# Far key products of a delta-rule scan moved from VectorE to GpSimd, in a one-core transformer block

## What is computed

```python
q, k, v, beta = split(layernorm(x) @ w_qkvb + b_qkvb)      # 16 heads of 16
k = k / max(norm(k), 1e-6)
def step(S, inp):                                          # S: 16x16 per batch and head
    retrieval = einsum("bhij,bhj->bhi", S, k_t)
    S = S + einsum("bhi,bhj->bhij", beta_t * (v_t - retrieval), k_t)
    return S, einsum("bhij,bhj->bhi", S, q_t)
x = x + (x + scan_out @ w_out + b_out)
```

## Time and profile before

| | before |
|---|---|
| time of 3 runs: median (lowest to highest) | 1209.48 us (1209.47 to 1211.79) |
| the profiled execution, its time | 1210.13 us |
| its span, first to last instruction | 1208.4 us |
| DVE busy | 999.9 us (83%) |
| PE busy | 947.1 us (78%) |
| ACT busy | 632.2 us (52%) |
| POOL busy | 438.6 us (36%) |

### The profile page before, as it was taken

The page is one execution under the profiler, slowest core; times in us unless marked ns, Lnnn a source line. Parts: engine busy times, 40 slices in busy tenths (PEclk is TensorE's granted clock), DMA queues, the critical chain, the costliest instruction groups (busy, mean ns, idle before and its releaser), DMA issues.

```text
span 1208.4 us, 19595 instructions
## 1 busy us (share of the span) xinstructions
PE 947.1 (78%) x6080; PEld 707.4 (59%) x6087; DVE 999.9 (83%) x3021; ACT 632.2 (52%) x1476; POOL 438.6 (36%) x647
## 2 busy tenths in 40 slices
PE   1468999999999999999999998899887601794156
PEld 1357777777777777777777776666655400341034
DVE  3578999999999999999999998855666788798877
ACT  1244555555555655655556553446476440684097
POOL 2413543535435445354353441314467640000000
PEclk9688999999999999999999998899998955797579
DMA  9430000000000000000000000133300000000012
GB/s 198 59 105 1 9 7 6 10 6 7 9 5 10 6 6 10 6 9 7 6 10 5 8 8 5 27 110 105 93 13 1 1 0 0 1 1 1 1 49 92
DMA packets 30263, 30.51 MB, mean 25 GB/s; under 512 B 7248, under 2 KB 25552, under 8 KB 30160
## 3 DMA queue, kind: packets, MB, share of 16 engines
q1 hardware_dynamic: 30160, 29.26, 9.5%
HBM read 20.85 MB, written 4.19 MB: 21 GB/s over the span
## 4 chain that ended last, share of the span: by engine, by line
DVE 61%; PE 24%; issue 9%; ACT 4%; POOL 1%; DMA 1%; DVEq 0%; SPq 0%; ACTq 0%; POOLq 0%
PE ps L1543 6%; DVE arena L993 6%; DVE arena L996 6%; DVE work L1477 4%; DVE arena L975 4%; DVE arena L974 4%; PE ps L1705 3%; DVE arena L984 3%; DVE arena L987 3%; DVE arena L1039 3%; PE psY L1726 3%; DVE work L901 2%; DVE arena L1046 2%; PE psX L1726 2%; DVE arena L997 2%
## 5 line engine op out<-in xcount | busy, mean ns | idle before, releaser
L482 POOL TENSOR_TENSOR arena<-arena 128x256 f32<-128x256 f32 x32 | 23.3, 728 | 367.2 <-DVE arena L975 367.2
L572 ACT ACTIVATE arena<-ps 128x512 f32<-128x512 f32 x128 | 72.9, 596 | 49.2 <-PE ps L1601 48.7
L537 ACT ACTIVATE arena<-ps,nparity 32x256 f32<-32x256 f32 x124 | 51.1, 457 | 81.8 <-PE ps L1543 81.4
L457 POOL TENSOR_SCALAR_AFFINE_SELECT arena<-arena 128x2048 f32<-128x2048 f32 x32 | 92.1, 2877 | 2.2
L1601 PE MATMUL ps<-work 32*128 32x256 f32 x512 | 91.8, 400 | 0.8 <-ACT w2t L642 0.7
L1543 PE MATMUL ps<-work,arena 128*128 128x64 f32 x496 | 68.1, 295 | 30.6 <-DVE work L1008 30.0
L1543 PEld LDWEIGHTS ps<-work,arena 128*128 128x128 f32 x496 | 63.4, 207 | 37.7 <-DVE work L1008 37.7
L1566 PE MATMUL psG<-arena 128*128 128x512 f32 x128 | 73.8, 659 | 1.9 <-DVE arena L1039 1.9
L468 POOL TENSOR_TENSOR work<-work 128x16 f32<-128x16 f32 x96 | 51.2, 533 | 58.1 <-DVEq L1068 53.1
L1601 PEld LDWEIGHTS ps<-work 32*128 32x128 f32 x512 | 61.1, 184 | 17.5 <-issue 10.1
L993 DVE TENSOR_TENSOR arena<-arena 128x256 f32<-128x256 f32 (+1 forms) x96 | 66.4, 692 | 3.3
(11 more groups left out here) (294 smaller groups left out, 2640.2 us busy)
## 6 DMA issues: line engine op xcount, KB each, us to landing
arena<-in_mask_BxSxS_ik SPq DMA_DIRECT2D x8, 1024.0 KB, 6.7
arena<-in_x SPq DMA_DIRECT2D x32, 128.0 KB, 11.9
arena<-in_ctx SPq DMA_DIRECT2D x8, 512.0 KB, 4.2
xs<-arena SPq DMA_DIRECT2D x256, 16.0 KB, 1.8
out<-xs SPq DMA_DIRECT2D x32, 128.0 KB, 1.7
arena<-in_L_ffn_w SPq DMA_DIRECT2D x2, 1024.0 KB, 8.8
arena<-in_L_attn_w_qkvb SPq DMA_DIRECT2D x1, 1024.0 KB, 8.8
work<-in_L_attn_w_out SPq DMA_DIRECT2D x1, 256.0 KB, 4.7
```

What stands on the lines that cost most here:

```text
L457: G.affine_select(out=pairs, in_=pairs, compare_op=ALU.is_ge, fill=0.0, base=0, pattern=[[0, NH], [-CT, B], [0, CT]], channel_multiplier=1 ...
L572: A.activation(attn[j % 2][:, r * 512:(r + 1) * 512], ps[(2, 0)[r % 2]][:, :], ACT.Copy).then_inc(att_out, 1)
```

## The change

`far_products` is taken out of DVE's program and written into POOL's. On POOL it is called at the end of each iteration j, for chunk j + 2, behind `key_norms(j + 3)`. It waits for the same two semaphores (`k_ready`, `g1_mm`), does the same multiplication from the same keys into the same columns of `PR`, and increments the same `prod1`. The helpers `over_s` and `over_t` are written out. Nothing else is changed; the orders of PE, ACT and SP stay.

```diff
@@ GpSimd @@
+            def far_products(m):
+                pool.wait_ge(k_ready, m + 1)
+                pool.wait_ge(g1_mm, 2 * m)
+                key = kq[m % 4][:, 0:CW].rearrange("p (q t) -> p q t", t=16)
+                late = key[:, :, 8:16].rearrange("p q (t a) -> p q t a", a=1).broadcast_to([P, NH, 8, 8])
+                early = key[:, :, 0:8].rearrange("p q (a s) -> p q a s", a=1).broadcast_to([P, NH, 8, 8])
+                G.tensor_tensor(PR[:, 0:1024].rearrange("p (q t s) -> p q t s", t=8, s=8), late, early,
+                                ALU.mult).then_inc(prod1, 1)
...
                     mask_attention(j)
                 if j + 3 < NCK:
                     key_norms(j + 3)
+                if 0 <= j + 2 < NCK:
+                    far_products(j + 2)
@@ VectorE @@
-            def far_products(m):
-                v.wait_ge(k_ready, m + 1)
-                v.wait_ge(g1_mm, 2 * m)
-                key = kq[m % 4][:, 0:CW].rearrange("p (q t) -> p q t", t=16)
-                V.tensor_tensor(PR[:, 0:1024].rearrange("p (q t s) -> p q t s", t=8, s=8),
-                                over_s(key[:, :, 8:16], 8), over_t(key[:, :, 0:8], 8), ALU.mult).then_inc(prod1, 1)
...
                     scale_near(j + 1)
-                if exists(j + 2):
-                    far_products(j + 2)
                 if exists(j + 2):
                     near_products(j + 2)
```

## The result

The changed kernel takes 1298.1 us (median of 4 runs, 1292.82 to 1300.44), the kernel before in the same comparison 1210.63 (1209.47 to 1216.0): a ratio of 1.0707, 95% interval 1.066 to 1.0754, 87 us slower. The forecast was 1271.5 us in a range of 1240 to 1306; sign and range held, and the time lies 26.6 us above the forecast. The profiled execution took 1299.14 us, with a span of 1297.4.

The account below looks back on a forecast made before the run. DVE and PE are both nearly full, so waits within one chunk decide. 21 chunks at +1.9 us and 8 at +2.6 average 2.1, times 29 is 61, plus 1 for filling: 1271.5 us, range 1240 to 1306.

Parts of the forecast that it names:

- The gap begins after the due time: POOL's idle gap opens at 439.22, but PE takes the far products at 437.95; PE would stand 3.1 us.
- Length of the product: The 128x1024 multiplication on POOL: taken as 2.2 us, with 1.9 and 2.9 as ends.
- Gain in the Newton rounds: POOL's Newton rounds wait less for DVE once L1039 is gone: 0.6 us gained, ends 0 and 1.36.
- Start of the product: On POOL, L475 ends at 438.6 and the product starts at 438.8, getting in between DVE's solve instructions.
- From the product's end to L1004: One far_gram half, the turn of the norms (L1587) and two handovers on PE before DVE's L1004: 1.6 us.
- the ring: L1004's delay passes through the solve, masks, seed and Newton rounds to the next product: every chunk 1.9 us longer.
- The lock: Two-SBUF-input DVE solve instructions stand for POOL's product: +2.6 us in 8 of 29 chunks; pacing all, 1303 us, chance 0.17.
- the main case: PE's turn of the norms waits behind POOL's product, with standing solve instructions covered: +1.9 us a chunk; chance 0.72.
- The clock: TensorE's granted clock in the scan was taken to hold, PE being busy 86%; the sum had no term for it.
- The fifth rival: PE's 3.1 us stands drop TensorE's clock from 0.98 to 0.76: 73 us more, 1344 us; chance 0.05.
- Play at L901: DVE's L901 stands until POOL's L457 ends; its 1.1 us of play take up PE's 0.35 us lateness.
- the forecast's queue: PE, in order, stands at far_gram for the product with norms_turned and the rest queued behind: +1.9 us a chunk.

Follow-up runs that it names:

- the filled kernel: The changed kernel with two matmuls of 512 columns added on PE ahead of its wait for the product: 1244.65 us (ratio 1.0273).
- the lock alone: The kernel before, DVE's L1039 kept, with the same product also formed on POOL into columns nobody reads: 1274.67 us (ratio 1.0525).
- the norms first: The changed kernel with norms_turned and the second pair of attention parts ahead of both far_gram halves on PE: 1259.51 us (ratio 1.0416).

## Why the prediction was right in its sign and short in its size

- *The gap begins after the due time*: right. POOL's idle time said nothing of when the product is needed. PE stood for it in every chunk of the scan from 120 to 760 us. The stand was put at 3.1 us and is 1.4 us on average in the changed kernel, where dips make PE late for it, and 437.28 - 434.91 = 2.4 us, filling and rest, in the filled one.
- *Length of the product*: taken 2.2 us, measured 1.95 (1959 ns mean), at the lower end kept, the line through the 128x16 row and the broadcast-input row. The estimate from the Trainium skill's 4497 ns (GPSIMD Engine Reference, Performance versus the Vector engine), 2.25 us, is further off.
- *Gain in the Newton rounds*: taken 0.6 us. From the first L468 to the end of L475 it was 439.22 - 433.87 = 5.35 us and is 435.32 - 430.83 = 4.49 in the filled kernel: 0.86.
- *Start of the product*: taken 0.2 us behind the end of L475, measured 0.04 us ahead of it (435.28 against 435.32).
- *From the product's end to L1004*: taken 1.6 us, measured 1.5 (437.23 to 438.73).
- With these four, 1.9 us a chunk becomes 439.22 - 0.86 - 0.04 + 1.95 + 1.5 - 440.71 = 1.06 us, and the sum 31 us in place of 62. The filled kernel, at full clock, measured 33 above the kernel before and 1.06 a chunk. Its period is the ring that the prediction closed.
- *The lock*: right as a row (1.87 us, ending with the product) and, in the filled kernel, mostly hidden, as said of the main case: L1017 waits 0.29 us for PE there. In the changed kernel itself the dips make PE's retrieval late far more often than in 8 of 29 chunks, and then it isn't hidden: in the chunk shown DVE waits 1.02 us for it at L1085, and L1017 starts at 461.20, 0.33 us after the turn has ended, held by the solve.
- *The clock*: the step that failed. The fifth rival had it at 0.05, and the sum had nothing for it; it cost 53 us. The argument against it compared mean shares: PE busy 88% of the attention stage at 0.97, so 86% in the scan would do. The changed kernel shows PE busy 93% (596.37 of 640) at 0.86, and the kernel before 94% at 0.97: the mean share does not tell them apart, partly because slow matmuls count as busy. What the change added was a new stand for the product in each chunk, 1.4 us on average, and that stand was in the prediction, at 3.1 us. Filling it brought the clock back. The rival's size, 73 us, came from the mean clock of another stage; its own row was 0.86 in place of 0.98.
- *Play at L901*: that L901's 1.1 us absorb a late PE was right at full clock (L914 still takes 1.29 us in the filled kernel) and used up with the dips (0.17 us).

The forecast's size erred both ways, the queue by 31 us too much and the clock by 53 too little. That the time lay inside the range is owed in part to the two errors having opposite signs: the forecast's queue and the measured clock together would have given 1271.5 + 53 = 1325 us. The upper end of the range, 1306, had been set for the lock and not for the clock.

## What to carry to other kernels

Before work is moved into an engine's idle time, look up when its consumer comes: a gap that opens after the due time is no room. On GpSimd, look also at what VectorE runs in that gap: here a two-input multiplication of 0.19 us stood 1.87 us behind a GpSimd product of 1.95, while a one-input reduction of 1.22 us beside it kept its time, so a product cut to fit beside the reduction held nothing up. One input is no general pass: L901, a `tensor_scalar`, stands until GpSimd's mask selection ends (1.28 us instead of 0.18). And a new stand on TensorE is to be priced with the work behind it at the lower clock level; a cheap matmul in the stand is the test, and sometimes the remedy.

## What the runs showed of the hardware that had not been expected

With PE standing 1.4 us for the product in each chunk (35.4 us in 26 chunks), its granted clock fell to half for 3.4 to 10.2 us at a time; with 2 us of matmuls in that stand it was 1.00 from 120 to 760 us instead of 0.86, with one matmul 0.95. In the kernel before, with a stand of 0.93 us in most chunks, it was 0.97. The length of the stand alone does not put the runs in order: 2.0 us a chunk went with 0.93 (the lock alone), 1.4 us with 0.86 (the changed kernel), and with the norms first some dips had no stand before them. On GpSimd a multiplication with one broadcast input took 1.07 us for 512 columns and 1.95 us for 1024, so 1.7 ns for each further column: 1.95 us lies on the line through the rows of 128x16 (0.21 us) and of 128x256 with two broadcast inputs (0.62 us), which gave 1.9.
